# Folded wavelet weights: kept in SBUF after the front convolution, stored beside the first token stage

## What is computed

```python
def _L0_conv_ref(x, w_in, w_dw, fft_w, w_out):
    x = jnp.einsum('oc,bchw->bohw', w_in, x)
    xp = x.reshape(B, C2, h, P, w, P).transpose(0, 1, 2, 4, 3, 5)
    xf = jnp.fft.rfft2(xp) * fft_w
    xp = jnp.fft.irfft2(xf, s=(P, P))
    x = xp.transpose(0, 1, 2, 4, 3, 5).reshape(B, C2, H, W)
    x = jax.lax.conv_general_dilated(x, w_dw, window_strides=(1, 1), padding='SAME', feature_group_count=C2, dimension_numbers=('NCHW', 'OIHW', 'NCHW'))
    x1, x2 = jnp.split(x, 2, axis=1)
    x = jax.nn.gelu(x1, approximate=False) * x2
    return jnp.einsum('oc,bchw->bohw', w_out, x)
...
def _L0_ffn_ref(x, W1, b1, W2, b2):
    h = jax.nn.relu(_qlinear(x, W1, b1))
    y = _qlinear(h, W2, b2)
    return y
...
    x = x + _L0_conv_ref(_ln_c(x), ...)
    t = _to_tokens(x)
    t = t + _L0_ffn_ref(_ln_t(t), ...)
    x = _from_tokens(t, x)
    x = x + _L1_conv_ref(_ln_c(x), ...)
    t = _to_tokens(x)
    t = t + _L1_ffn_ref(_ln_t(t), ...)
    x = _from_tokens(t, x)
```

## Time and profile before

| | |
|---|---|
| median of 3 runs | 2622.57 us |
| lowest and highest | 2621.44 and 2628.5 us |
| the profiled execution | 2624.89 us, span 2623.1 us |
| PE, DVE, ACT, POOL busy over the span | 87%, 58%, 43%, 17% |
| front convolution, first to last block on PE | 373.5 to 807 us |
| first token stage, first projection to last | 827.08 to 1261 us |
| DMA over the span | 458.55 MB, 175 GB/s |

### The profile page before, as it was taken

One profiled execution on the slowest core, in us unless ns is written; L12 is line 12 of the kernel. 1 busy time (PEld: TensorE's weight loads), 2 busy tenths in 40 slices (PEclk: granted clock), 3 DMA queues, 4 the chain that ended last, 5 costly groups with the idle time before them and its releaser, 6 DMA issues. The chain is left out here.

```text
span 2623.1 us, 62156 instructions
## 1 busy us (share of the span) xinstructions
PE 2272.7 (87%) x21290; PEld 1247.5 (48%) x21290; DVE 1523.5 (58%) x2653; ACT 1123.3 (43%) x2338; POOL 450.0 (17%) x707
## 2 busy tenths in 40 slices
PE   6679778898996999999699999999976998688886
PEld 3344436667773333333266666666641232233332
DVE  3345401111113777777488888888842455577776
ACT  4346421111112888888532222222211111577776
POOL 7510015100100000000054444444410000000000
PEclk9789869999997999999899999999987999899999
DMA  6999989788874777877576666666628999333332
GB/s 154 260 254 270 253 284 303 230 263 262 285 245 91 142 142 146 152 142 145 100 155 144 142 142 142 142 143 143 144 86 162 240 267 237 87 102 106 105 102 78
DMA packets 533239, 458.55 MB, mean 175 GB/s; under 512 B 316476, under 2 KB 445444, under 8 KB 529778
## 3 DMA queue, kind: packets, MB, share of 16 engines
q1 hardware_dynamic: 462882, 425.87, 63.4%
q0 software_dynamic: 5744, 23.34, 3.7%
q10 hardware_dynamic: 64512, 7.88, 2.3%
HBM read 272.33 MB, written 186.40 MB: 175 GB/s over the span
## 5 line engine op out<-in xcount | busy, mean ns | idle before, releaser
L604 PE MATMUL gate_ps<-gate_data,gate_wt 64*64 64x289 f32 x6144 | 397.1, 416 | 39.2 <-issue 27.2
L604 PEld LDWEIGHTS gate_ps<-gate_data,gate_wt 64*64 64x64 f32 x6144 | 303.1, 136 | 134.3 <-issue 59.8
L662 DVE TENSOR_TENSOR gate_out<-gate_gelu,gate_ps 128x578 f32<-128x578 f32 x96 | 72.2, 756 | 399.3 <-PE gate_ps L604 343.7
L949 ACT CAST mix_h<-mix_bank 96x512 f16<-96x512 f32 x512 | 267.6, 593 | 7.1 <-PE mix_bank L900 3.2
L639 ACT ACTIVATE gate_gelu<-gate_ps 128x578 f32<-128x578 f32 x96 | 62.7, 653 | 367.8 <-PE gate_ps L604 331.2
L2036 PE MATMUL fus_bank<-fus_xt,fus_taps 76*32 76x512 f32 x1344 | 159.6, 626 | 28.4 <-DMA fus_shift<-gate_shift 23.5
L1031 DVE TENSOR_SCALAR mix_hb<-mix_h,mix_b1q 96x1024 f16<-96x1024 f16 x256 | 122.7, 479 | 93.6 <-ACT mix_h L949 93.6
L900 PE MATMUL mix_bank<-mix_xq,mix_w1q 112*96 112x512 fp8e5 x512 | 143.5, 382 | 29.1 <-ACT mix_h L949 23.0
L1039 DVE CAST mix_hq<-mix_hb 96x2048 fp8e5<-96x2048 f16 x128 | 156.5, 1223 | 19.5 <-DVE mix_hb L1031 16.9
L292 DVE COPY exp_out<-exp_y 128x384 f32<-128x384 f32 x192 | 102.1, 567 | 103.5 <-PE exp_y L255 52.1
L912 PE MATMUL mix_x_bank<-mix_hq,mix_w2q 96*112 96x512 fp8e5 x512 | 136.1, 388 | 29.9 <-DVE mix_hq L1039 27.7
(11 more groups left out here) (226 smaller groups left out, 4050.6 us busy)
## 6 DMA issues: line engine op xcount, KB each, us to landing
y<-exp_out SPq DMA_DIRECT2D x64, 816.0 KB, 12.2
gate_data<-y SPq DMA_DIRECT2D x24, 2176.0 KB, 17.6
g<-gate_out SPq DMA_DIRECT2D x48, 578.0 KB, 4.9
mix_sc<-g SPq DMA_DIRECT2D x31, 816.0 KB
gate_wt<-wm SPq DMA_DIRECT2D x96, 256.0 KB, 8.5
wav_strips<-xp SPq DMA_DIRECT2D x96, 204.0 KB, 3.8
wav_halves<-xp SPq DMA_DIRECT2D x48, 340.0 KB
init<-wav_init SPq DMA_DIRECT2D x48, 268.0 KB, 2.4
```

Of the source, the lines that this page charges most:

```text
L604: mm = pe.matmul(banks(a, v)[64 * g:64 * (g + 1), r], wt[q][64 * r:64 * (r + 1), 2 * a + g, n, :], src, start=n == 0, stop=n == 3)
L949: act.copy(h16[at.pair][:, m, h, :], bank[(2 * m + h) % len(bank)][0:HID, :]).then_inc(h16_ready, 1)
```

## The change

`stage` and `part` become buffers `tab["stage"]` and `tab["part"]`, which live until the end of the first token stage. `wavelet_weights` keeps its first half, up to the spreading of level 0 into `stage`, and has no `pace` inside; ahead of it stands one wait for four blocks (`out_ready` at 10). So the wait that was ahead of the zeros is now ahead of the 21 loads and the `wav_low` copy too. The six stores, and the clearing and spreading of level 1 between them, form the new function `wavelet_stores`, which GpSimd runs in `mix0`, where `pace(n)` waits for `x2_ready` at 4 + 6n, that is for 6n steps; n is 1 and 2 for `wav_front`, 3 to 6 for `wav_lines`. On SP a wait for the gate constants stands behind their load.

```diff
-        stage = k.sb("stage", [HID, len(JOBS), 2 * NT])
+        stage = tab["stage"]
...
                 sp.dma_start(maps[:, :], t["cg_maps"]).then_inc(maps_in, 16)
+                sp.wait_ge(maps_in, 16)
                 load_weights(0, 0)
...
-                wavelet_weights(nc, pool, t, tab, k, stage, lambda n: pool.wait_ge(out_ready, 2 + 8 * n))
+                pool.wait_ge(out_ready, 2 + 8)
+                wavelet_weights(nc, pool, t, tab, k)
...
+            if tab is not None:
+                @block.gpsimd
+                def _(pool):
+                    wavelet_stores(pool, t, tab, k, lambda n: pool.wait_ge(x2_ready, SLOTS + 6 * n))
...
     chain.link(pool.memset(zero[:, :, :], 0.0))
-    pace(1)
...
+def wavelet_stores(pool, t, tab, k, pace):
+
+    room, part = tab["stage"][0:C].rearrange("c j w -> c (j w)"), tab["part"]
+    lines1 = room[:, 0:80 * LINE1].rearrange("c (v t x) -> c v t x", v=4, t=20)
+    step, weights_out = k.sem("fold_step"), k.sem("fold_out")
+    chain = Chain(pool, step, 0)
     for r in range(2):
-        pace(2 + r)
-        pool.dma_start(t["wav_front"][:, r, :, 2 * STRIP:7 * STRIP], image0[:, :, :, :].rearrange("c p t i -> c p (t i)")
-                       ).then_inc(weights_out, 16)
-    pool.wait_ge(weights_out, 16 * 6)
+        pace(1 + r)
+        pool.dma_start(t["wav_front"][:, r, :, 2 * STRIP:7 * STRIP],
+                       room[:, 0:K0 * 5 * STRIP].rearrange("c (p w) -> c p w", p=K0)).then_inc(weights_out, 16)
+    pool.wait_ge(weights_out, 16 * 2)
     chain.link(pool.memset(lines1[:, :, :, :], 0.0))
...
     for q in range(4):
         at = q * 4 * 20 * LINE1 + 4 - q
-        pace(4 + q)
+        pace(3 + q)
         pool.dma_start(t["wav_lines"][:, at:at + 4 * 20 * LINE1 - 4], flat[:, 4:]).then_inc(weights_out, 16)
-    pool.wait_ge(weights_out, 16 * 10)
+    pool.wait_ge(weights_out, 16 * 6)
...
-        gated_conv(nc, t, tab)
-        token_mix(nc, t, "mix0", t["g"], t["woutT"], None, t["x"], t["w1T_0"], t["b1_0"], t["w2T_0"],
-                  t["b2_0"], t["x2"], t["xp"])
+        with ExitStack() as folding:
+            for name, shape in (("stage", [HID, 10, 2 * NT]), ("part", [C, 2, 4, 5, 4, 5, 4])):
+                tab[name] = folding.enter_context(nc.sbuf_tensor(f"tab_{name}", shape, F32))
+            gated_conv(nc, t, tab)
+            token_mix(nc, t, "mix0", t["g"], t["woutT"], None, t["x"], t["w1T_0"], t["b1_0"], t["w2T_0"],
+                      t["b2_0"], t["x2"], t["xp"], tab)
```

More of the change, by code:

```diff
@@ L669, in _, with token_mix @@
                 pool.wait_ge(gates_out, 16 * 2 * len(JOBS))
-                wavelet_weights(nc, pool, t, tab, k, stage, lambda n: pool.wait_ge(out_ready, 2 + 8 * n))
+                pool.wait_ge(out_ready, 2 + 8)
+                wavelet_weights(nc, pool, t, tab, k)
                 pool.wait_ge(fuse_ready, 1)
                 wavelet_tables(pool, tab, k)
-def token_mix(nc, t, tag, src, wT, bias, res, w1T, b1, w2T, b2, dst, norm_dst):
+def token_mix(nc, t, tag, src, wT, bias, res, w1T, b1, w2T, b2, dst, norm_dst, tab=None):
     N = HW // NT
@@ L1132, in wavelet_tables, with wavelet_weights @@
     chain.link(x)
-def wavelet_weights(nc, pool, t, tab, k, stage, pace):
-    room = stage[0:C].rearrange("c j w -> c (j w)")
+def wavelet_weights(nc, pool, t, tab, k):
+    room, part = tab["stage"][0:C].rearrange("c j w -> c (j w)"), tab["part"]
     zero = room[:, 0:TOP * 2 * B * XW].rearrange("c (y w) -> c y w", y=TOP)
@@ L1141, in wavelet_weights @@
     outer = k.sb("outer", [C, 2, 4, 4, 4])
-    part = k.sb("part", [C, 2, 4, 5, 4, 5, 4])
     image0 = room[:, 0:K0 * 5 * STRIP].rearrange("c (p t i) -> c p t i", t=5, i=STRIP)
-    lines1 = room[:, 0:80 * LINE1].rearrange("c (v t x) -> c v t x", v=4, t=20)
     tables_in, step, weights_out = k.sem("tables_in"), k.sem("pool_step"), k.sem("weights_out")
@@ L1191, in wavelet_weights @@
     chain.link(x)
+def wavelet_stores(pool, t, tab, k, pace):
+    room, part = tab["stage"][0:C].rearrange("c j w -> c (j w)"), tab["part"]
+    lines1 = room[:, 0:80 * LINE1].rearrange("c (v t x) -> c v t x", v=4, t=20)
+    step, weights_out = k.sem("fold_step"), k.sem("fold_out")
+    chain = Chain(pool, step, 0)
     for r in range(2):
-        pace(2 + r)
-        pool.dma_start(t["wav_front"][:, r, :, 2 * STRIP:7 * STRIP], image0[:, :, :, :].rearrange("c p t i -> c p (t i)")
-                       ).then_inc(weights_out, 16)
-    pool.wait_ge(weights_out, 16 * 6)
+        pace(1 + r)
+        pool.dma_start(t["wav_front"][:, r, :, 2 * STRIP:7 * STRIP],
+                       room[:, 0:K0 * 5 * STRIP].rearrange("c (p w) -> c p w", p=K0)).then_inc(weights_out, 16)
+    pool.wait_ge(weights_out, 16 * 2)
     chain.link(pool.memset(lines1[:, :, :, :], 0.0))
     for y in range(5):
-        x = pool.tensor_copy(lines1[:, :, :, LINE1 // 2 + 2 - y], ready[:, 1, y].rearrange("c v x o -> c v (x o)"))
+        x = pool.tensor_copy(lines1[:, :, :, LINE1 // 2 + 2 - y],
+                             part[:, 1, 0, y].rearrange("c v x o -> c v (x o)"))
     chain.link(x)
-    flat = lines1[:, :, :, :].rearrange("c v t x -> c (v t x)")
+    flat = room[:, 0:80 * LINE1]
     for q in range(4):
         at = q * 4 * 20 * LINE1 + 4 - q
-        pace(4 + q)
+        pace(3 + q)
         pool.dma_start(t["wav_lines"][:, at:at + 4 * 20 * LINE1 - 4], flat[:, 4:]).then_inc(weights_out, 16)
-    pool.wait_ge(weights_out, 16 * 10)
+    pool.wait_ge(weights_out, 16 * 6)
 def everywhere_all(table, name):
```

## The result

| | before | after |
|---|---|---|
| median, us | 2625.53 (4 runs) | 2649.14 (4 runs, 2645.07 to 2666.79) |
| ratio after to before, 95% interval | | 1.0102 [1.0052, 1.0153] |
| profiled execution, us | 2624.89 | 2645.07 (span 2643.3) |
| gate constants and front convolution, first to last matmul | 465.4 | 436.0 |
| token stage `mix0`, first to last matmul | 463.7 | 520.1 |

The change makes the kernel 1.0% slower: 2625 was forecast, 2640 was the upper end. The front convolution gives what was forecast, -29.4 us against -29.9. The token stage takes 56.4 us, not 33. The two make +27.0. In this execution the start, up to the first matmul of the gates, was 3.5 us longer and the fusion stage, where nothing was changed, 8.9 us shorter; with -1.3 elsewhere that is the 20.2 us of the spans.

A forecast was written before the change was run, and what follows sets the result against it. Front convolution stalls of 54.5 us, partly from GpSimd stores shutting out SP's queue, were to be removed: -34.4 + 5 - 0.5 + 33 = +3.1 us, so 2625 us, no measurable change; range 2604 to 2640.

The forecast's parts named there:

- Front convolution, -34.4: Front convolution: without the six stores, three long loop turns save 19.4 us and the g buffer waits 15.0 us.
- Displaced copies, +5: Front convolution: constants' loads and wav_low copy start later, at about 409 us, costing 0 to 10.3 us, taken as 5.
- SP's wait, -0.5: Start of the gates: the constants load alone, gaining 0 to 1.2 us, taken as 0.5; later loads stay hidden.
- Memset beside DVE, 0: Token stage: GpSimd's memset between the stores, now beside a busy DVE, costs 0, with 4.9 us as upper bound.
- Token stage, +33: Token stage: six stores each delay the mix_sc load by their engine time; 20 to 36.6 us, taken as 33.
- Nothing suggests that a late projection is made up: Token stage: steps follow each other at 6.93 us, so a late projection's delay stays in the total.
- A: Rival, faster: in the token stage q1 keeps running beside q0, so stores cost 20 us or less; 2613 us, chance 0.31.
- B: Rival, slower: displaced copies sit on the first data load, so the first turn stays long; 2638 us, chance 0.27.
- C: Rival: SP's new wait makes the front convolution's first block late, needing an 18 us slip; given no chance of its own.

The follow-up runs named there:

- early_copies: The kernel after, with the 21 constant loads and the wav_low copy again ahead of the wait for the fourth block; one run, 2665.0 us.
- before_again: The kernel before, unchanged, profiled a second time; one run, 2618.8 us.
- shifted_stores: The kernel before, with GpSimd's steps in the front convolution each released two blocks later; one run, 2605.0 us.
- shifted_and_wait: The kernel before, with GpSimd's front-convolution steps released two blocks later and SP's wait on the gate constants added; 2596.0 us, ratio 0.9881.
- quarter_stores: The kernel after, with each of the six stores cut into four, 24 in all, each released by an odd step; 2645.8 us, ratio 1.0070.
- best_even_half: The kernel after, with twelve half-size stores released by even steps and the constants' copies ahead of the fourth-block wait again; 2611.2 us, ratio 0.9953.

## Why the prediction was wrong, step by step

- **Front convolution, -34.4.** Right in size and in cause: with the stores gone the stalls go. Without the displaced copies (early_copies) the excess is 20.7 us in place of 54.5, a gain of 33.8. But it was read from one execution: before_again had 46.9, against which the gain is 26. The base alone was uncertain by 8 us, and a store on a turn is no sure sign of a long turn, as that execution shows. Some luck was in the hit.
- **Displaced copies, +5.** Right: 25.8 - 20.7 = 5.1.
- **SP's wait, -0.5.** The constants gained 0.96 us; nothing was lost. What else it may bring is open, 3 to 5 us by the three pairs (5.4 and 3.4 less than before_again, 2.8 between shifted_stores and shifted_and_wait).
- **Memset beside DVE, 0.** Right in after, by luck of place. Elsewhere the same memset cost the 4.9 us that stood as the upper bound. That no cast of DVE lay beside GpSimd was too narrow a look: the instruction that was held is a `TENSOR_SCALAR`.
- **Token stage, +33.** The step that failed, mis-sized: it measured 56.4. The place, the six stops and the load they wait for were right. The price was q0's own time, 5.8 or 6.7 us a store, and called an upper bound. It isn't one, for two reasons. First, TensorE, stopped for 5.8 to 8.7 us, went on at 1.2 GHz and was late again in the following step: 16.9 us by its busy time (quarter_stores, with short stops, has 35.2 us in all). Second, SP's transfers go out in one order, and what stands ahead of `mix_sc` was held as well: the waits are 39.5 us, for the two `wav_front` stores most of all (the first of the two late steps 8.7 and 8.5 us over, where 6.2 was taken). So of the 23 us that the term was short, 17 are the lower clock, which the sum had at nothing, and 6 are longer waits. That SP's order is the reason is read from the rows alone; no kernel changed it.
- **"Nothing suggests that a late projection is made up"** was right, and the sentence should have gone on: what does a stop do to the step after it? The trace of before had a case. Behind the barrier ahead of the token stage TensorE begins at the lower clock:

```profile
827.00:839.00 12.00, 9.46 (x22) 2.94 (x22) 2.27 (x5) 1.91 (x3) 0.00 (x0) 0.50 0.63 109
```

- **Rivals.** A (shared queues, 20 us) is out; it held only for stores in the other phase and of half the size, 7 us. B is out by its own sign, the first turn (10.09 us, not 18), though its long first `g` wait was there. C did not happen. The slower outcome came from none of them, but from the main forecast's largest term.

The forecast set a gain of 30 against a loss of 33 with the loss bounded at 36.6, so that no case reached 2649. With the 16 to 17 us that the lower clock costs behind six stops, it would have been 2642, outside the stated range and within 7 us of the median.

## What to carry to other kernels

A background transfer costs by where it starts, more than by its bytes or the stage it lies in: find the stretch just behind the load that the loop waits for, and cut the transfer until what is queued on the loading engine is through before the next load is due. Cutting alone does not do it: halves in the phase of after cost 59.6 us, halves in the other phase 7. When you price a late load for TensorE, add the step that follows the stop, at the lower clock, and count every transfer that stands ahead of the load in its issuing engine's program. Cut long GpSimd memsets when they lie beside DVE's 16-bit work.

## What the runs showed of the hardware

- After stops of 2.49, 2.66 and 5.76 us TensorE's next matmuls took up to twice their time (1.96 in place of 1.07 us), and so they did behind stops of 1.46 to 1.95 us in quarter_stores; behind its stops of about 1 us, and one of 1.56 in best_even_half, they did not. Each of the former costs the step it lies in or the following one 1 to 3 us.
- While q0 moves a `wav_lines` store (48 rows of 23 KB), SP's issue of a small store goes from 0.89 to 3.75 us for two, and that of the `mix_sc` load from 0.34 to 3.18. Without any store, two small loads right behind a `mix_sc` load take 3.23 in place of 0.88.
- A GpSimd memset of 4.89 us held one f16 `TENSOR_SCALAR` of DVE for 4.98 in place of 0.48 us; 16 memsets of 48x360 held one to 0.78.
- A stage that keeps all DMA engines full (fusion) took 216.5 to 245.6 us for the same instructions and bytes, at 258 and 228 GB/s.
- The next 16 KB of instructions moved 7 us later when they came behind the first packets of a GpSimd store than when they came ahead of them (450.87 and 443.55 us), and the loop turned that much later.
